# Two decoder layers on one core: first phase rebuilt around the PSUM banks, with softplus on VectorE and one capped exponential

## What is computed

```python
x = x + mamba(layernorm(x))                 # 32 heads of 16, state 128
x = x + cross_attention(layernorm(x), ctx)  # 16 heads, mask of the context
x = x + moe(layernorm(x))                   # shared expert + top 2 of 16
# mamba, per sequence, written as the kernel does it:
xs = silu(conv4(x @ Wx) + conv_b)           # causal, per channel
dt = softplus(x @ Wdt + dt_bias); cum = cumsum(-exp(A_log) * dt)
M[h, s, t] = exp(cum[h, t] - cum[h, s]) * (B[s] . C[t])   for s <= t, else 0
y = sum_s M[h, s, t] * dt[s, h] * xs[s] + D[h] * xs[t]
out = (rmsnorm(y) * silu(z)) @ Wout
```

## Time and profile before

| what | value |
|---|---|
| runs | 4787.19, 4792.0, 4794.8 us, median 4792.0 |
| span of the profiled execution | 4774.6 us |
| busy PE / DVE / ACT / POOL | 88 / 70 / 60 / 57% of the span |
| first loop, its once-a-body tanh | from 40.6 to 2374.5 us, 64 bodies |

### The profile page before, as it was taken

The page is one execution under the profiler, slowest core; times in us unless marked ns, Lnnn a source line. Parts: engine busy times, 40 slices in busy tenths (PEclk is TensorE's granted clock), DMA queues, the critical chain, the costliest instruction groups (busy, mean ns, idle before and its releaser), DMA issues.

```text
span 4774.6 us, 119919 instructions
## 1 busy us (share of the span) xinstructions
PE 4215.5 (88%) x34006; PEld 3007.4 (63%) x34071; DVE 3359.3 (70%) x8668; ACT 2885.5 (60%) x7026; POOL 2721.2 (57%) x4093
## 2 busy tenths in 40 slices
PE   5888888888888888888869979999999999999998
PEld 3666555665565565665547756666666666666665
DVE  4667666777767766667635557777777787777776
ACT  3666666666666666666634446666666666666564
POOL 5666666666666666666622335555555555555554
PEclk8989999999999999999979989999999999999999
DMA  3222232222222222222224401111111111111110
GB/s 112 89 88 89 95 103 78 75 75 98 76 75 75 85 88 76 75 75 84 89 67 144 133 24 32 31 31 31 31 31 30 29 30 31 29 30 31 31 31 18
DMA packets 222142, 304.10 MB, mean 64 GB/s; under 512 B 56720, under 2 KB 175760, under 8 KB 222096
## 3 DMA queue, kind: packets, MB, share of 16 engines
q1 hardware_dynamic: 197632, 249.83, 16.7%
q0 software_dynamic: 19200, 52.45, 3.4%
q10 hardware_dynamic: 5264, 1.25, 0.1%
HBM read 239.19 MB, written 64.23 MB: 64 GB/s over the span
## 4 chain that ended last, share of the span: by engine, by line
PE 58%; DVE 19%; issue 11%; POOL 6%; ACT 4%; DMA 1%; DVEq 1%; ACTq 1%; POOLq 1%; SPq 0%
PE Q L1427 21%; PE Q L1432 10%; PE Q L1420 5%; PE Q L1470 4%; DVE arena L832 4%; DVE arena L830 3%; PE Q L1777 3%; PE Q L1810 3%; PE Q L1629 3%; PE Q L1461 3%; PE Q L1455 2%; DVE arena L860 2%; DVE mx L782 2%; PE Q L1641 2%; POOL arena L640 1%
## 5 line engine op out<-in xcount | busy, mean ns | idle before, releaser
L1432 PE MATMUL Q<-ident,arena 128*128 128x128 f32 x4768 | 803.8, 292 | 155.3 <-ACT arena L1176 69.4
L1432 PEld LDWEIGHTS Q<-ident,arena 128*128 128x128 f32 x4768 | 557.2, 146 | 390.1 <-issue 146.0
L1427 PE MATMUL Q<-Wkvl,arena 128*128 128x512 f32 x1024 | 500.3, 601 | 0.0
L640 POOL TENSOR_TENSOR arena<-arena 128x1024 f32<-128x1024 f32 x256 | 479.5, 1890 | 14.3 <-DMA arena<-cum_rows 14.3
L704 POOL TENSOR_TENSOR l<-l,half_pow 128x8 f32<-128x8 f32 x192 | 318.5, 1659 | 233.0 <-DVE l L1057 231.2
L729 POOL TENSOR_TENSOR arena<-arena,part_of 128x512 f32<-128x512 f32 x256 | 263.8, 1041 | 190.8 <-DVE part_of L1095 190.6
L782 DVE TENSOR_REDUCE mx<-Q 128x4 f32<-128x512 f32 x512 | 344.0, 682 | 11.3 <-PE Q L1455 6.6
L1470 PE MATMUL Q<-arena 128*17 128x128 f32 x4096 | 244.5, 312 | 115.5 <-ACT arena L1193 115.5
L1461 PE MATMUL Q<-ident,arena 128*128 128x128 f32 x2048 | 301.4, 280 | 13.2 <-ACT arena L1193 11.4
L1461 PEld LDWEIGHTS Q<-ident,arena 128*128 128x128 f32 x2048 | 231.4, 142 | 122.9 <-issue 75.7
L1186 ACT ACTIVATE arena<-Q,mx 128x128 f32<-128x128 f32 x1024 | 281.8, 373 | 1.0 <-DVE mx L782 1.0
(11 more groups left out here) (311 smaller groups left out, 10677.9 us busy)
## 6 DMA issues: line engine op xcount, KB each, us to landing
arena<-cum_rows SPq DMA_DIRECT2D x256, 512.0 KB, 6.6
arena<-routed_rows SPq DMA_DIRECT2D x144, 128.0 KB, 2.1
expert_rows<-arena POOLq DMA_DIRECT2D x144, 128.0 KB, 2.0
arena<-in_x_dram SPq DMA_DIRECT2D x128, 128.0 KB, 5.0
arena<-in_ctx_dram SPq DMA_DIRECT2D x128, 128.0 KB, 6.6
x_rows<-arena SPq DMA_DIRECT2D x128, 128.0 KB, 1.7
arena<-x_rows SPq DMA_DIRECT2D x128, 128.0 KB, 2.4
out_dram<-arena SPq DMA_DIRECT2D x64, 128.0 KB, 1.7
```

Source lines behind the costliest of these rows:

```text
L640: tell(g.tensor_tensor(E8[j], E8[j], cums[:, 8 * j:8 * j + 8].unsqueeze(2).broadcast_to([P, 8, T]), ALU.subtract), "diff")
L1427: last = mm(out, lhs(c), rhs(c), start=c == 0, stop=c == n - 1)
L1432: last = nc.tensor.transpose(out[:, c * P:(c + 1) * P], src[:, c * P:(c + 1) * P], ident[:, :])
```

## The change

Convolution: ACT writes the last tap with the bias straight from bank Q[1]; DVE adds the other three, each from the bank with a shifted range; the padded tile goes. C.B is masked from bank to bank (Q[4]), and all four products are DVE's, with the bank as their second operand. The decay exponents: POOL subtracts and, in chunks 0 and 1, caps at zero in eight instructions a chunk with a scalar for each partition; chunk 2 is subtracted whole and capped in a second instruction; chunk 3 keeps Abs on ACT. ACT takes Exp directly in 0 to 2. x dt is laid out in pairs of 32 columns, half of them zero, so that the 32 heads go to Q[3] by channel, two accumulating matmuls for each 32 channels; the transposes and bank copies of y go, y2 is made by channel with D as a per-partition scalar (`Dch`, eight small loads in place of one), the sum of squares by PE. z and the shared expert's hidden are computed transposed. Softplus is DVE's altogether, as a chain of 14. `centre` has three instructions. The chain W (norm, query) is apart from X and uses bank Q[2]. The attention's maxima are no longer subtracted by DVE. Routing finds both experts in one sorted maximum of the logits. Both `awake` calls go. ORDER[1] is new.

The core of the diff:

```diff
         "SP": """
-Ncb0 Ncb1 Ncb2 Yc Xm Mx Ncb3 Nx Mco Fm Fo
+Ncb0 Mx Ncb1 Ncb2 Xm Yc Ncb3 Nx Mco Fm Fo
         """,
         "POOL": """
-Nd0 Nd1 Nd2 Xx1r Fln3 Xln2 Mln1 Nd3 Msp Nm3 Fsc Nyg Nrms
+Nd0 Nd1 Nd2 Mln1 Fln3 Wln2 Nd3 Fsc Nyg Nrms Wx1r
         """,
         "DVE": """
-Fln3 Xln2 Nm0 Mln1 Fr Yk Ftop Mdt Fslot Msp Xm0 Xm1 Fhg Nm1 Nm2 Xm2 Xm3 Fxo Vcv Vcv1 Vcv2 Vcv3 Ny0 Vxs2 Ny1 Vcb Vxdt Vgz Nx1 Xho
+Mln1 Fln3 Nm0 Wln2 Yk Nm1 Nm2 Mdt Fr Ftop Fslot Msp Msp6 Msp4 Msp2 Msp0 Fhg Nm3 Fxo Xm0 Xm1 Ny Xm2 Nss Xm3 Vcv1 Vcv2 Vcv3 Nx1 Vxs2 Vcb Vxdt Xho Vgz
         """,
         "ACT": """
-Ng0 YcT Ne0 Ng1 Fln3 Xln2 Fln3n Xmr Xln2n Mln1 Frx Mln1n Xq Mab Vbc Ne1 Ng2 Yv Fth Ne2 Ng3 FhT Ne3 Xm0 Xm1 Vxp Xm2 Mcum Xm3 NYt0 Xt0 NYt1 Xt1 Vcth Xt2
-Xt3 Nsq XOT NyT Vtz
+YcT Ne0 Ne1 Xmr Ne2 Mln1 Fln3 Mln1n Yv Fln3n Wln2 Mab Wln2n Frx Ne3 Wq Fth Ne4 Mcum Vbc Xm0 Xm1 Nsq Vcv Xm2 Xm3 Xt0 Xt1 Xt2 Vcth Xt3 XOT Vtz
         """,
         "PE": """
-YcT Yk Nv0 Fln3n Yv Xln2n Fr Mln1n Xq Vbc Mdt Frk Xs0 Fgu Fguh Vip1 Vip1h FhT Xs2 Fdn Mcum Nv1 Nv2 Xt0 Nv3 Xt1 Ny0 Xt2 VCB Ny1 Xt3 Xpv Xpv0 VxsT Xpv1
-Xpv2 NyT Xpv3 Vz Vzh Npr Nprh XOT
+YcT Yk Yv Mln1n Fln3n Mdt Fr Wln2n Nv0 Nv1 Frk Wq Fgu Fguh Xs0 Mcum Fdn Vbc Nv2 Nv3 Vip1 Vip1h Xs2 Nss Npr VCB Xt0 Xt1 Xt2 Nprh Xt3 Xpv Xpv0 VxsT Xpv1 Xpv2
+Xpv3 Vz XOT Vzh
         """,
     },
     3: {
...
         done(pool, f"wide{j}", b, 16)
-        tell(g.tensor_tensor(E8[j], E8[j], cums[:, 8 * j:8 * j + 8].unsqueeze(2).broadcast_to([P, 8, T]), ALU.subtract), "diff")
-    yield "m3"
-    done(pool, "E", b, 4)
-    done(pool, "cbm", b)
-    tell(g.tensor_tensor(E8[3], E8[3], cbm.unsqueeze(1).broadcast_to([P, 8, T]), ALU.mult), "M3")
+        if j < 2:
+            pool.sem_inc(SEM["passed_Pool"], 1)
+            for i in range(8):
+                last = g.tensor_scalar(E8[j][:, i, :], E8[j][:, i, :], cums[:, 8 * j + i:8 * j + i + 1], 0.0, ALU.subtract, ALU.min)
+        else:
+            last = g.tensor_tensor(E8[j], E8[j], cums[:, 8 * j:8 * j + 8].unsqueeze(2).broadcast_to([P, 8, T]), ALU.subtract)
+            if j == 2:
+                link(pool, "N_POOL", b, last, bare=True)
+                last = g.tensor_scalar(Ew[j], Ew[j], 0.0, None, ALU.min)
+        tell(last, "diff")
     yield "yg"
     done(pool, "y2", b)
     tell(g.tensor_tensor(yg, gz, y2, ALU.mult), "yg")
     yield "rms"
-    done(pool, "ss", b)
-    link(pool, "N_POOL", b, g.tensor_tensor(ss0[:, 1:2], ss0[:, 0:1], eps[:, 1:2], ALU.add))
+    done(pool, "ssv", b)
     tell(g.tensor_tensor(ss0[:, 2:3], ss0[:, 1:2], half_pow[:, 0:1], ALU.pow), "rms")
-def X(b):
+def W(b):
+    yield "ln2"
+    centre("ln2", mvX, b, "W_POOL")
     yield "x1r"
-    done(pool, "x1", b)
     was(pool, "x2", b)
     tell(g.tensor_tensor(x1r, x1, bv0b[:, :], ALU.add), "x1r")
-    yield "ln2"
-    centre("ln2", mvX, b, "X_POOL")
 def F(b):
     yield "ln3"
...
+    s, z, tail_of = dts[:, 2, :], dts[:, 3, :], dts[:, 4, :]
+    J(v.tensor_tensor(s, u, dts[:, 5, :], ALU.mult))
+    J(v.tensor_tensor(z, s, s, ALU.mult))
+    J(v.tensor_scalar(tail_of, z, 2.0 / (2 * TERMS - 1), None, ALU.mult))
+    for k in range(TERMS - 2, 0, -1):
+        if k % 2 == 0:
+            yield f"sp{k}"
+        J(v.scalar_tensor_tensor(tail_of, tail_of, 2.0 / (2 * k + 1), z, ALU.add, ALU.mult))
+    yield "sp0"
+    J(v.scalar_tensor_tensor(tail_of, tail_of, 2.0, s, ALU.add, ALU.mult))
+    J(v.scalar_tensor_tensor(dts[:, 6, :], dts[:, 0, :], 0.0, tail_of, ALU.max, ALU.add))
...
-    yield "cv"
-    done(dve, "xpad", b)
-    for k in range(NCONV):
-        if k:
-            yield f"cv{k}"
+    for shift in range(1, NCONV):
+        yield f"cv{shift}"
+        if shift == 1:
+            done(dve, "conv0", b)
         for c in range(IC):
-            src, wk = xpad[:, c, k:k + T], convw[:, c, k:k + 1]
-            out = xc[:, c * T:(c + 1) * T]
-            if k == 0:
-                last = v.scalar_tensor_tensor(out, src, wk, convb[:, c:c + 1].broadcast_to([P, T]), ALU.mult, ALU.add)
-            else:
-                last = v.scalar_tensor_tensor(out, src, wk, out, ALU.mult, ALU.add)
-        if k < NCONV - 1:
+            late = xc[:, c * T + shift:(c + 1) * T]
+            k = NCONV - 1 - shift
+            last = v.scalar_tensor_tensor(late, Q[1][:, c * T:(c + 1) * T - shift], convw[:, c, k:k + 1], late, ALU.mult, ALU.add)
+        if shift < NCONV - 1:
             J(last)
...
     done(dve, "CB", b)
-    was(dve, "M3", b)
-    tell(v.tensor_tensor(cbm, Q[1][:, 0:T], triu[:, :], ALU.mult), "cbm")
+    tell(v.tensor_tensor(Q[4][:, 3 * T:4 * T], Q[4][:, 2 * T:3 * T], triu[:, :], ALU.mult), "cbm")
     yield "xdt"
     done(dve, "xsT", b)
     done(dve, "a", b)
     was(dve, "Yk", b, 4)
-    was(dve, "y2", b)
-    v.tensor_tensor(heads(xdt), heads(Q[1][:, :]), wide(dts[:, 6, :]), ALU.mult)
-    tell(v.tensor_tensor(heads(xD), heads(Q[1][:, :]), wide(Dpb[:, :]), ALU.mult), "xdt")
+    tell(v.tensor_tensor(pairs(xdt), Q[1][:, :].rearrange("p (i k w) -> p i k w", k=2, w=HP),
+                         dts[:, 6, :].rearrange("p (i k) -> p i k", k=2).unsqueeze(3).broadcast_to([P, NH // 2, 2, HP]), ALU.mult), "xdt")
     yield "gz"
     done(dve, "tz", b)
     was(dve, "yg", b)
     tell(v.scalar_tensor_tensor(gz, tz, 1.0, Q[1][:, :], ALU.add, ALU.mult), "gz")
 def N(b):
-    for j in range(3):
+    for j in range(4):
         yield f"m{j}"
         done(dve, "E", b, j + 1)
-        tell(v.tensor_tensor(E8[j], E8[j], cbm.unsqueeze(1).broadcast_to([P, 8, T]), ALU.mult), "M")
-    for half_ in range(2):
-        yield f"y{half_}"
-        done(dve, "Yb", b, half_ + 1)
-        o = slice(half_ * DI // 2, (half_ + 1) * DI // 2)
-        last = v.tensor_tensor(heads(y2[:, o]), Q[3 + half_][:, :].rearrange("p (h w) -> p h w", w=32)[:, :, 0:HP],
-                               heads(xD[:, o]), ALU.add)
+        done(dve, "cbm", b)
+        tell(v.tensor_tensor(E8[j], E8[j], Q[4][:, 3 * T:4 * T].unsqueeze(1).broadcast_to([P, 8, T]), ALU.mult), "M")
+    yield "y"
+    done(dve, "Yk", b, 4)
+    done(dve, "xs2", b)
+    for c in range(IC):
+        o = slice(c * T, (c + 1) * T)
+        last = v.scalar_tensor_tensor(y2[:, o], th0[:, o], Dch[:, c:c + 1], Q[3][:, o], ALU.mult, ALU.add)
     tell(last, "y2")
+    yield "ss"
+    done(dve, "ss", b)
+    tell(v.tensor_scalar(ss0[:, 1:2], Q[3][:, D:D + 1], 16.0 * RMS_EPS, None, ALU.add), "ssv")
     yield "x1"
     done(dve, "mamba", b)
     done(dve, "rms", b)
...
+    moments("ln2", x1, stX, mvX, "W_DVE", b)
+
 def X(b):
     banks = (Q[5], Q[6], Q[5], Q[6])
-    yield "ln2"
-    done(dve, "x1", b)
-    moments("ln2", x1, stX, mvX, "X_DVE", b)
-    yield from scores(b, banks, S0, mx0, 0, "X_DVE")
+    for j in range(4):
+        yield f"m{j}"
+        done(dve, "S0", b, j + 1)
+        tell(v.tensor_reduce(mx0[:, 4 * j:4 * j + 4], banks[j][:, :].rearrange("p (g k) -> p g k", g=NG), AX.X, ALU.max, negate=True), "S0max")
     yield "ho"
     done(dve, "PV0", b, 2)
-    link(dve, "X_DVE", b, headout(b, Q[6], rc0, o0, "X_DVE"))
+    pv = Q[6][:, :].rearrange("p (h w) -> p h w", w=32)
+    link(dve, "X_DVE", b, v.reciprocal(rc0[:, :].unsqueeze(2), pv[:, :, AW:AW + 1]))
+    link(dve, "X_DVE", b, v.tensor_tensor(pv[:, :, 0:AW], pv[:, :, 0:AW], rc0[:, :].unsqueeze(2).broadcast_to([P, AH, AW]), ALU.mult))
     done(dve, "x1r", b)
     was(dve, "xo", b)
-    tell(v.tensor_tensor(x2, x1r, o0, ALU.add), "x2")
+    tell(v.tensor_tensor(across(x2), pv[:, :, 0:AW], across(x1r), ALU.add), "x2")
 cell = [0]
...
-    tell(v.tensor_reduce(rt[:, 0, 0:1], Q[7][:, D:D + NE], AX.X, ALU.max, negate=True), "rmax")
+    dve.sem_inc(SEM["passed_DVE"], 1)
+    logits, top = Q[7][:, D:D + NE], rt[:, 3, 0:8]
+    J(v.max(top, logits), bare=True)
+    J(v.max_index(rti[:, 0, :], top, logits))
+    tell(v.tensor_scalar(rt[:, 0, 0:1], top[:, 0:1], -1.0, None, ALU.mult), "rmax")
+    for k in range(2):
+        last = v.scalar_tensor_tensor(sel[:, k, :], iota[:, :], rti[:, 0, k:k + 1], ones[:, 0:NE], ALU.is_equal, ALU.mult)
+    J(last)
+    tell(v.tensor_tensor(selb[:, :], sel[:, 0, :], sel[:, 1, :], ALU.add), "sel")
     yield "top"
     done(dve, "rexp", b)
     was(dve, "meta_out", b, 16)
     J(v.reciprocal(rt[:, 0, 2:3], rt[:, 0, 1:2]))
-    J(v.tensor_tensor(rt[:, 2, :], rt[:, 1, :], rt[:, 0, 2:3].broadcast_to([P, NE]), ALU.mult), bare=True)
-    J(v.max(rt[:, 3, 0:8], rt[:, 2, :]), bare=True)
-    J(v.max_index(rti[:, 0, :], rt[:, 3, 0:8], rt[:, 2, :]))
...
-    J(v.scalar_tensor_tensor(sel[:, 0, :], iota[:, :], rti[:, 0, 0:1], ones[:, 0:NE], ALU.is_equal, ALU.mult))
-    J(v.scalar_tensor_tensor(rt[:, 5, :], sel[:, 0, :], -2.0, rt[:, 2, :], ALU.mult, ALU.add), bare=True)
-    J(v.max(rt[:, 6, 0:8], rt[:, 5, :]), bare=True)
-    J(v.max_index(rti[:, 1, :], rt[:, 6, 0:8], rt[:, 5, :]))
-    J(v.scalar_tensor_tensor(sel[:, 1, :], iota[:, :], rti[:, 1, 0:1], ones[:, 0:NE], ALU.is_equal, ALU.mult))
-    tell(v.tensor_tensor(selb[:, :], sel[:, 0, :], sel[:, 1, :], ALU.add), "sel")
```

(69 more changed lines are left out.)

184 lines of the change are left out of this document (86 added, 98 removed).

## The result

The kernel after takes 4897.9 us (median of 4 runs, 4896.4 to 4902.4) against 4791.6 for the kernel before (4 runs too, the three of the table and 4791.2): 1.0226 times as long, 95% interval 1.0212 to 1.0241. It is 2.3% slower, where 4545 us and faster was forecast. The profiled execution went from a span of 4774.6 to 4894.8 us.

What follows compares the result with a forecast made beforehand. The first loop was taken as bound by a path hopping between five queues; 63 gaps times (37.05 - 33.1) is 249 us, with set-up and ends -247, so 4792.0 goes to 4545 us, range 4445 to 4690.

Steps and rivals of the forecast that it cites:

- the price of the caps: GpSimd, chunks 0 to 2: 0.37 us per capped 128x128 subtraction, 1.3 for the wide cap, 9.2 us instead of 5.6.
- the 1.6 of cover: GpSimd between bodies: 1.6 us of slack hide the caps; anything beyond comes onto the path through ln1 and ln3.
- the caps are slow: Rival, GpSimd chunks 0 to 2: 1.04 us per cap, 19.8 us of chunks, a 40.4 us cycle, 5005 us; chance 0.06.
- the path list: First loop: eleven steps across the engines, adding up to a 32.05 us body at full clock, against 35.90.
- the clock: TensorE in the first loop: low-clock stretches without fillers add 1.0 us, making the body 33.1.
- step 1: Body start, 0 to 6.2 us: DVE without a pause on moments, three products, key add and dt add.
- step 2: Routing, to 8.9 us: Fr 1.5, rank on PE 0.25, top and slot 1.0; before, about 5 us.
- step 3: DVE, to 13.0 us: softplus 3.3 and gate products 0.85, ahead of the shared expert's product.
- step 7: DVE, to 24.7 us: max 0.68, sum of squares 0.2, max 0.6, 12 taps at 0.285.
- step 11: Body end, to 32.05 us: tanh of z on ACT 0.65, gz on DVE 0.65.
- The clock is the price: Rival, TensorE: two low stretches per body with all 3.4 us on the path, 35.45 a body, 4690 us; chance 0.20.
- The quarrel of VectorE and GpSimd: First loop: the two engines hold each other up where both read two SBUF operands; first tap 2.4 to 3.3 us, 1.2 free.

Runs made afterwards that it cites:

- the best kernel: The kernel after with chunks 0 to 2 subtracted whole on GpSimd and their Abs on ACT at the end of the body before: 4503.3 us, 0.9399 of before.

## Why the prediction was wrong

**The step that failed is the price of the caps**, and it fails as a size, not as a mechanism. It said 0.37 us for a capped subtraction, with bounds 0.29, 0.46 and 1.04, and 1.1 to 1.9 for the wide cap, taken at 1.3. Measured: 0.71 and 2.78. The first lies within the bounds, the second above its upper end. Chunks 0 to 2 are 16.4 us where 9.2 stood. Put only this into the prediction's own sum: 7.2 us more, less the 1.6 of cover, is 5.6 a body; 33.1 becomes 38.7, against 39.04 measured, and 4528 becomes 4528 + 63 x 5.6 = 4881 of the measured span of 4894.8. By this sum the one term holds 353 of the 367 us of the miss. The table of chunks and bodies says the same without the sum: 9.2 us of chunks lie under its bend at 9.9, where the body is that of the kernel without caps, which takes 4489.6 us; no kernel with 9.2 us was run.

How it went wrong can be told from the rows themselves. For 128x128 I went from a 128x32 instruction's best time to a two-input one's (L618, 0.456), and took it that one wide input costs less than two. For the wide cap the same thought gave L640's 1.89 as the upper bound. The trace held no GpSimd instruction that read a scalar from a tile or did two operations at this width; the experiments have them: 0.60 for one operation, 0.71 for two, 2.77 for 128x1024 with one input against 1.90 with two. On that engine the number of inputs was no guide. The kernel before did hold a second width of L630's form (one input, one operation with a constant), in phase 3, which neither the rows nor the prediction used:

```profile
L705 POOL TENSOR_SCALAR l<-l x192: 240/240/265, 2797.1 to 4736.4; 128x8 f32<-128x8 f32 x192
```

From 0.240 us at 8 columns and 0.291 at 32 a line gives 0.50 at 128 and 2.4 at 1024, an estimate. That makes some 12.2 us of chunks where 9.2 was taken, and a body of 34.5 by the prediction's own sum: still too little, but the wide cap would have stood above a subtraction, not below it. The prediction's own figure for dearer caps also does not follow from its cover: at 0.46 us each they add 16 x 0.09 = 1.4 us, less than the 1.6 of cover, and not 0.8 to the body.

**The rival "the caps are slow"** had the mechanism and 0.06. It decides from 0.82 us an instruction, it said, with 3.2 us for chunk 2: from 16.4 us of chunks (16 x 0.82 + 3.2 = 16.3), which is what they take. Yet the body is 39.04, not 37.05, as its cycle was 20.6 us around the chunks and is 22.7. About 0.8 us of that lies from the first centre step to the end of the logits: 5.6 us in the kernel after (1230.34 to 1235.94), 4.8 in the kernel without caps (1227.16 to 1231.97), 4.7 in the rival's own sum. PE does this stretch with the clock at 0.51 in the kernel after; the four matmuls of the logits take 1.01 us there, and in the kernel without caps:

```profile
1231.35 0.62 PE L1402 MATMUL Q<-Wr,arena 128*128 128x16 f32 x4
```

The other 1.3 us lie behind the logits, where PE is slow until 1242; how much of them is the clock was not isolated. By the measured prices the rival alone would have given 16.4 + 20.6 = 37.0, no change; its form was right, its constant 2 us short and its chance too small. So the prediction's two sums part here: the path list plus 5.6 gives 38.7, with 1.0 for the clock in it, and the cycle gives 37.0 with nothing for the clock. That the first comes within 0.4 of 39.04 is partly luck, since the cycle is what bounds the kernel after.

**The path list was right.** It said 32.05 plus 1.0 for the clock; the body without caps takes 32.57, the best kernel 32.86. DVE's timeline in the kernel without caps, in a body of the shorter size, answers to its steps (zero at 1226.33, the next zero at 1258.04):

```profile
1226.33 0.42 DVE L734 BATCH_NORM_STATS2 stM<-arena 128x6 f32<-128x256 f32 x1
...
1232.34 0.18 DVE L778 TENSOR_TENSOR arena<-Q,dtb 128x32 f32<-128x32 f32 x1
...
1235.12 0.18 DVE L948 TENSOR_REDUCE meta<-rt 128x2 uint32<-128x32 f32 x1
...
1238.88 0.42 DVE L954 SCALAR_TENSOR_TENSOR arena<-Q,arena 128x256 f32<-128x256 f32 x1
...
1247.57 3.41 DVE L806 SCALAR_TENSOR_TENSOR arena<-Q,convw,arena 128x127 f32<-128x127 f32 x12
...
1257.44 0.69 DVE L826 SCALAR_TENSOR_TENSOR arena<-arena,Q 128x512 f32<-128x512 f32 x1 [0.24 <-ACT arena L1210]
```

| ends | listed at | measured at |
|---|---|---|
| step 1, dt add (L778) | 6.2 | 6.2 |
| step 2, slot (L948) | 8.9 | 9.0 |
| step 3, gate products (L954) | 13.0 | 13.0 |
| step 7, taps (L806) | 24.7 | 24.7 |
| step 11, gz (L826) | 32.05 | 31.8 |

More points that the kernel after confirms, in the source row of the taps and in DVE's timeline: 12 bank-fed taps at 0.28 us each with none stretched, the last sum of the routing under 2 us after its first link, the product with a bank operand no dearer than L860 in the earlier trace rows. (A tap's row says 0.340, as the taps overlap in time.)

```profile
L814 DVE SCALAR_TENSOR_TENSOR arena<-Q,convw,arena x768: 333/340/351, 42.4 to 2505.1; 128x127 f32<-128x127 f32 x64, 128x126 f32<-128x126 f32 x64, 128x125 f32<-128x125 f32 x64
```

```profile
1213.13 3.41 DVE L814 SCALAR_TENSOR_TENSOR arena<-Q,convw,arena 128x127 f32<-128x127 f32 x12
...
1236.10 0.18 DVE L938 MAX8 rt<-Q 128x8 f32<-128x16 f32 x1 [0.75 <-PE Q L1412]
...
1237.19 0.17 DVE L944 TENSOR_TENSOR selb<-sel 128x16 bf16<-128x16 f32 x1
```

1237.36 - 1236.10 is 1.26 us where the earlier trace rows has 3.95. L814's longest is 0.351, where L830 reached 3.25 for four, 0.81 each. The measured 1.215 and 1.219 of the same product with and without a bank operand go against the surcharge that the Trainium skill, VectorE: DVE Perf Modes, section "The TRN2 errata", would have put on bank operands.

**The clock** was the term that I trusted least. "The clock is the price" (4690, 0.20) is no explanation: it asked for a body of 35.45, and the body without caps takes 32.57, with no fillers either. The term itself, 1.0 us, was about right. With the clock's two levels at 1 and 0.5, the shorter body of the kernel without caps (0.95) has 3.2 us at 1.2 GHz, the longer one (0.90) 6.6. In the shorter one shown they lie beside DVE's first steps, which end as listed; the longer one takes 1.3 us more. So there one stretch costs next to nothing, and the second 1.3 us in about every other body: 32.57 - 31.73 = 0.8 us on average. The prediction's 1.65 "of a body as things stand" was such a difference between two sizes too; on average the kernel before lost 37.05 - 35.90 = 1.15.

**The quarrel of VectorE and GpSimd** was stated too narrowly, as one "where both read two SBUF operands": L630 and L602 have one tensor input each and are held up all the same.

**The signs** did their work, all but one. "Cap instructions over 0.5 us" and "a granted clock of 0.5 over more than 7 us of a body" are in the rows after, and DVE pauses in step 1:

```profile
1231.49 1.22 DVE L841 TENSOR_TENSOR arena<-arena,Q 128x1024 f32<-128x1024 f32 x1 [3.07 <-ACT arena L1228]
```

That pause was to mean that the logits come last; here it is ACT's Exp of chunk 2, behind the wide cap. "ACT's first Exp waiting for GpSimd" did not come: the second and the third wait.

## What to carry to other kernels

Before work moves to an engine, look whether the trace holds that form of instruction there (inputs, scalar operand, operations, width); where it doesn't, compute the cover first, and if the upper bound breaks it, give the slow side a real chance. Two widths of one form give at least a line. Here 1.6 us of cover, rightly found within 1 us, stood against 7.2 us of mispriced work. And place a moved instruction against all that stands behind it in its queue: the same three Abs cost 233 us more ahead of the norms than at the end of the body before.

## What the runs showed of the hardware

- GpSimd with one tensor input is not cheap: 128x1024 capped at a constant takes 2.77 us, the subtraction with two inputs at the same width 1.90. The Trainium skill, GPSIMD Engine Reference, section "4.1 Engine selection", has two-input operations about twice as slow as on VectorE and one-input ones near line rate; for these two forms the trace has the order the other way round.
- Its 128x128 instruction with a per-partition scalar: 0.60 us with one operation, 0.71 with two. Eight of them (5.7) are dearer than one subtraction and one wide cap (4.9).
- DVE products with two SBUF operands hold even a 128x1 GpSimd instruction until they end: 0.27 becomes 2.33 us for L602 with mvF and 0.99 with mvM, in the median. With a bank as one operand it is 0.27 again, and the product takes 1.215 us instead of 1.219. The Trainium skill, GPSIMD Engine Reference, section "1. Specifications", names this contention; its size here, 193 us on 4503, is that of the runs.
- Filler matmuls for the clock cost 1.4 to 1.6 us of a body and left the granted clock at 0.85 and 0.92, as it was.
